# Moving the next batch row's norm statistics into the FFN's first steps, and the FFN's first low part ahead of the second half's mixer addition

## The chip, the cores and the metric

The kernel runs on one core of one Trainium2 chip. The metric is the device time of one execution in microseconds (us). Before the change it is 1379.34 us, the median of 3 runs (1378.56 to 1380.21). The engines are named as the profile names them: PE is TensorE (PEld its weight loads), DVE is VectorE, ACT is ScalarE, POOL is GpSimd, SP is SyncE, which issues most of the DMA transfers.

## What is computed

Four batch rows of 512 tokens by 256 features go through four residual layers: a Mamba2 mixer, an FFN with weights quantized to -1, 0, 1, a causal attention with ALiBi biases, and a mixture of 64 experts. The two layers that the change touches are the first two:

```python
x = x + _L0_attn_ref(_layernorm(x), ...)   # mixer: ... g * rsqrt(mean(g * g) + EPS) * norm_w, then W_out
x = x + _L0_ffn_ref(_layernorm(x), w1, w2, w3)

def _layernorm(x, axis=-1, eps=1e-05):
    m = jnp.mean(x, axis=axis, keepdims=True)
    v = jnp.var(x, axis=axis, keepdims=True)
    return (x - m) / jnp.sqrt(v + eps)

# inside _L0_ffn_ref, with quantized weights
x1 = _bitlinear(x, w1)
x2 = _bitlinear(x, w2)
hidden = jax.nn.sigmoid(x1) * x2
return _bitlinear(hidden, w3)
```

## The kernel before, in words

The order of the work is written out by hand for each engine. Each engine runs its own list of instructions strictly in that order, and the lists meet in semaphores: `at(s, k)` makes the engine wait until signal `s` has been given `k` times in the current batch row `b`; `row(r)` switches `b`, so that a step of the coming batch row can stand among the steps of the present one. The four batch rows go one after the other through mixer, FFN and attention; the experts come at the end for all of them. Tokens are in four tiles of 128 (`T = 4`), and two tiles make a half (`p_` is 0 or 1).

Five normalizations of this kind exist, numbered `n`: 0 ahead of the mixer (its input in `pob`, statistics in `hstats`, `hmv`), 1 ahead of the FFN (`xb`, `stats`, `mv`), 2 ahead of the attention, 3 ahead of the experts. Each goes through four engines:

- `norm_stats(n, t)` on DVE: `bn_stats` of a tile (L1628), then `bn_aggr` (L1630);
- `norm_rstd(n, tiles)` on POOL: add epsilon (L2117), power -0.5 (L2118), for each tile in turn;
- `norm_apply(n, t)` on DVE (L1635): subtract the mean, multiply;
- `norm_T` on PE (L1083) turns a half, and `norm_copy` on ACT (L761) brings it out of PSUM.

For normalization 1 the copy on ACT writes the fp16 high part of the turned activations, and `low_part(p_)` on DVE (L1717) writes what it leaves over. PE's first FFN product waits for `low_part(0)`, and its products from step 6 on for `low_part(1)`.

The end of the mixer does, for each half: `mean_of_squares` (DVE, L1712), the root of it (POOL, L2189, signal `rms_rstd`), `add_mixer` (DVE, L1723 before: two instructions that add the mixer's output to `xb`), statistics and application of normalization 1. POOL takes the means and the statistics in the order in which `mixer_steps` on POOL lists them.

The FFN has 12 steps `n` (six tiles of the hidden layer for each half). In each, PE makes the up products (L1273, 8 matmuls), ACT the sigmoid (L880), DVE the product with the other branch (L1785, "hid" below), ACT its fp16 high part (L882), DVE the low part (L1788), and PE, two steps later, the down products (L1283, 4 matmuls). DVE's product of step `n` comes behind its low part of step `n - 1`. At step 8 DVE adds the first half's FFN output and starts normalization 2.

In batch rows 0 to 2 there is a coming row, whose normalization 0 is done in the shadow of all this. Batch row 3 has none: it runs the same code without the steps of a coming row.

Of the kernel before, what the change touches and what calls it, by code (L numbers as in the profile page):

```python
# [27 lines left out]
T = L // P  # L28
# [95 lines left out]
def build(nc, a, per_row):  # L124


    with ExitStack() as ctx:
# [1474 lines left out]
        def _(dve):  # L1602
# [5 lines left out]
            def at(s, k):  # L1608
                dve.wait_ge(s.sem, s.upto(k, b))

            def row(r):
                nonlocal b
                b = r
# [103 lines left out]
                h_lo_done.inc(v.tensor_tensor(h_lo[:, :, cols], pb[p_][:, :].rearrange("p (k n) -> p k n", k=KD), h_hi[:, :, cols], ALU.subtract))  # L1717

            def add_mixer(p_):
                at(rms_rstd, p_ + 1)  # L1720
                at(out_mm, T * (G - 1) + 2 * p_ + 2)
                for t in range(2 * p_, 2 * p_ + 2):
                    po_read.inc(v.scalar_tensor_tensor(out=xb[:, t, :], in0=pb[6 + p_][:, (t % 2) * D:(t % 2 + 1) * D], scalar=rms[:, t:t + 1],  # L1723
                                                       in1=xb[:, t, :], op0=ALU.mult, op1=ALU.add))
                if p_ == 1:
                    low_part(0)
                for t in range(2 * p_, 2 * p_ + 2):
                    at(po_read, t + 1)
                    norm_stats(1, t)

            def mixer_steps(coming):
                here = b
                for s in range(LAST):
                    _, early, late, _ = ahead_of(s)
                    if s + 1 < UNITS:
                        decays(s + 1, 0)
                    halves_of_y(s)
                    if s + 1 < UNITS:
                        decays(s + 1, 1)
                    gated(s)  # L1740
                    for tile in early:
                        if tile[0] == "x":
                            convolve(tile)
                    if s % T < T - 1:
                        grow_state(s)
                    for tile in late:
                        if tile[0] == "x":
                            convolve(tile)
                at(x_loaded, 1)
                for p_ in range(2):  # L1750
                    mean_of_squares(p_)
                    add_mixer(p_)
                    if coming is not None:
                        row(coming)
                        if p_ == 0:
                            dve.wait_ge(xnext_loaded.sem, xnext_loaded.upto(coming + 1))
                        for t in range(2 * p_, 2 * p_ + 2):
                            norm_stats(0, t)
                        row(here)
                    for t in range(2 * p_, 2 * p_ + 2):  # L1760
                        norm_apply(1, t)

            def ffn(coming):
                here = b
                for n in range(2 * FT):
                    p_, f = divmod(n, FT)
                    if coming is not None and n < T:
                        row(coming)
                        norm_apply(0, n)
                        row(here)  # L1770
                    if n == 3:
                        low_part(1)
                    if n == FT + 2:
                        for t in range(2):
                            add_ffn(t)
# [269 lines left out]
            for r in range(B):  # L2045
                coming = r + 1 if r + 1 < B else None
                row(r)
                mixer_steps(coming)
                ffn(coming)
                first_queries(coming)  # L2050
                attention(coming)
# [44 lines left out]
        def _(pool):  # L2096
# [6 lines left out]
            def row(r):  # L2103
                nonlocal b
                b = r
# [41 lines left out]
            def mixer_steps(done, coming):  # L2147
# [38 lines left out]
                for p_ in range(2):  # L2186
# [1 line left out]
                    settle(pool)  # L2188
                    rms_rstd.inc(p.tensor_tensor(rms[:, 2 * p_:2 * p_ + 2], msv[:, 2 * p_:2 * p_ + 2], power[:, 2 * p_:2 * p_ + 2], ALU.pow))  # L2189
                    norm_rstd(1, [2 * p_, 2 * p_ + 1])  # L2190
                    if coming is not None:
                        row(coming)
                        norm_rstd(0, [2 * p_, 2 * p_ + 1])
                        row(here)

            def maxima_parts(g):
                t, q = AGROUPS[g]
# [145 lines left out]
```

## Time and profile before

| | |
|---|---|
| median of 3 runs | 1379.34 us (1378.56 to 1380.21) |
| profiled execution | 1377.98 us, its span 1376.2 us |
| PE busy | 1146.5 us, 83% of the span |
| DVE busy | 906.0 us, 66% |
| ACT busy | 657.7 us, 48% |
| POOL busy | 585.4 us, 43% |
| mean granted clock of PE | 0.947 of full |

The span runs from the first to the last instruction that the profile shows; the execution's own time is 1.8 us longer. A busy share is an average over very different stages. The change lies in three stretches of about 25 us, one in each of the batch rows 0 to 2 (from about 203, 502 and 799 us on), and in a smaller way in batch row 3 (from 1099 us), so it has to be read from the order of time there.

### The profile page before, as it was taken

Reading aid. Unit: us, or ns where it says so; the run is one execution under the profiler, and the core shown is the slowest. Engines: PE = TensorE matmul, PEld = TensorE weight load, DVE = VectorE, ACT = ScalarE, POOL = GpSimd, SP = SyncE. Lnnn points to the kernel's source line nnn. Section 1 sums busy time; section 2 is a strip of 40 time slices with the busy share of each in tenths; the row PEclk is TensorE's granted clock in tenths of the full one; section 3 lists DMA queues with packets and bytes.
Section 4 is the critical chain, followed back from the end, with each engine's and each line's share of the span. In section 5 each row is a group of like instructions: output and inputs, shape, how many; then the busy total and the mean of one; then the engine's idle time right before and its main releaser. Section 6 shows DMA issues by size and latency. Waiting matters only on the chain.

```text
span 1376.2 us, 24576 instructions
## 1 busy us (share of the span) xinstructions
PE 1146.5 (83%) x8422; PEld 735.4 (53%) x8422; DVE 906.0 (66%) x1846; ACT 657.7 (48%) x1576; POOL 585.4 (43%) x789
## 2 busy tenths in 40 slices
PE   3799997888899978988899978989899978879940
PEld 2355565665555546655555656655555656654520
DVE  4488876655778866655887865656888755561417
ACT  3655523665454515666544335656544245621630
POOL 1254562220387761210677832200777612234750
PEclk9999998999999999998999999999999999989975
DMA  7365542300243304100343332001333525076879
GB/s 311 119 204 195 182 129 73 93 3 20 86 152 113 110 25 118 47 6 31 120 138 109 103 74 70 25 21 44 124 124 114 187 73 162 9 263 205 158 131 370
DMA packets 120139, 159.58 MB, mean 116 GB/s; under 512 B 11632, under 2 KB 82928, under 8 KB 119280
## 3 DMA queue, kind: packets, MB, share of 16 engines
q1 hardware_dynamic: 105232, 129.64, 30.0%
q0 software_dynamic: 9216, 19.98, 5.6%
q10 hardware_dynamic: 5568, 8.39, 1.7%
q8 instruction: 69, 1.13, 0.4%
q14 instruction: 54, 0.44, 0.1%
HBM read 104.55 MB, written 40.83 MB: 106 GB/s over the span
## 4 chain that ended last, share of the span: by engine, by line
PE 46%; DVE 19%; POOL 12%; issue 9%; ACT 8%; DMA 3%; ACTq 1%; POOLq 0%; SPq 0%; DVEq 0%
PE bank L1160 12%; DVE pool_c L1659 5%; PE bank L1202 4%; PE bank L1083 3%; POOL joint L2138 3%; DVE joint L1675 3%; PE bank L1381 3%; PE bank L1340 3%; PE bank L1366 3%; POOL xn L2145 2%; PE bank L1465 2%; PE bank L1305 2%; ACT joint L830 2%; DVE pool_c L1700 2%; PE bank L1181 2%
## 5 line engine op out<-in xcount | busy, mean ns | idle before, releaser
L1160 PE MATMUL bank<-xm,joint 128*128 128x512 f32 x544 | 272.0, 625 | 21.4 <-DVE pool_c L1659 15.6
L2138 POOL TENSOR_TENSOR joint<-joint 128x512 f32<-128x512 f32 x128 | 168.4, 1317 | 246.8 <-DVE joint L1675 246.2
L1659 DVE SCALAR_TENSOR_TENSOR pool_c<-bank,params,pool_c 128x511 f32<-128x511 f32 (+2 forms) x216 | 161.2, 747 | 86.6 <-ACT pool_c L791 81.2
L1160 PEld LDWEIGHTS bank<-xm,joint 128*128 128x128 f32 x544 | 99.8, 197 | 125.8 <-issue 93.3
L1851 DVE TENSOR_REDUCE nmax<-bank 128x1 f32<-128x384 f32 (+3 forms) x176 | 109.6, 638 | 57.3 <-PE bank L1341 56.5
L830 ACT ACTIVATE joint<-bank,dt_ 128x64 f32<-128x64 f32 x512 | 111.7, 342 | 31.1 <-PE bank L1083 31.1
L1202 PE MATMUL bank<-wout,pool_c 128*128 128x256 f32 x512 | 121.8, 381 | 1.2 <-DVE pool_c L1700 1.2
L1202 PEld LDWEIGHTS bank<-wout,pool_c 128*128 128x128 f32 x512 | 95.9, 190 | 33.7 <-issue 22.2
L2132 POOL DMA_INDIRECT xslot<-xrow,slots x96 | 97.0, 1010 | 34.9 <-issue 20.4
L800 ACT ACTIVATE pool_c<-pool_c 128x512 f32<-128x512 f32 x64 | 40.3, 629 | 135.8 <-DVE pool_c L1659 135.8
L1700 DVE TENSOR_TENSOR pool_c<-xn,pool_c 128x512 f32<-128x512 f32 x64 | 90.0, 1406 | 21.5 <-POOL xn L2145 21.5
L953 ACT ACTIVATE pool_c<-bank 128x512 f32<-128x512 f32 (+1 forms) x156 | 83.1, 550 | 17.8 <-PE bank L1368 15.6
L2117 POOL TENSOR_SCALAR vare<-mv 128x1 f32<-128x1 f32 x48 | 9.3, 194 | 190.0 <-DVE mv L1630 186.7
L1675 DVE TENSOR_TENSOR_SCAN joint<-pool_b,bank 128x512 f32<-128x512 f32 x64 | 77.6, 1213 | 17.1 <-POOL pool_b L2172 17.1
L1083 PE MATMUL bank<-consts,pool_c 128*128 128x128 f32 (+1 forms) x368 | 65.1, 278 | 22.3 <-DVE pool_c L1659 15.3
L1181 PEld LDWEIGHTS bank<-joint 128*64 128x64 f32 x1024 | 54.6, 136 | 53.3 <-issue 27.8
L1181 PE MATMUL bank<-joint 128*64 128x128 f32 x1024 | 70.0, 279 | 10.8 <-POOL joint L2138 10.8
L842 ACT ACTIVATE pool_c<-pool_c 128x512 f32<-128x512 f32 x64 | 40.6, 634 | 78.0 <-DVE pool_c L1700 78.0
L791 ACT ACTIVATE pool_c<-bank,params 128x512 f32<-128x512 f32 x72 | 56.4, 783 | 42.7 <-PE bank L1160 42.4
L2145 POOL TENSOR_TENSOR xn<-xn 128x512 f32<-128x512 f32 x48 | 60.8, 1267 | 32.3 <-DVE xn L1688 32.3
L1273 PE MATMUL bank<-pool_c,ffnw 128*128 128x256 f16 x384 | 58.7, 307 | 17.8 <-DVE pool_c L1717 14.0
L1340 PE MATMUL bank<-joint 108*128 108x128 bf16 (+3 forms) x256 | 68.9, 303 | 4.9 <-DVE nmax L1851 4.4
(272 smaller groups left out, 2399.6 us busy)
## 6 DMA issues: line engine op xcount, KB each, us to landing
pool_b<-dA_rows SPq DMA_DIRECT2D x64, 256.0 KB
pool_b<-dec_rows SPq DMA_DIRECT2D x96, 128.0 KB, 3.5
joint<-pool_b SPq DMA_DIRECT2D x96, 128.0 KB, 2.4
acc<-xrow SPq DMA_DIRECT2D x13, 640.0 KB, 6.1
joint<-dA_rows SPq DMA_DIRECT2D x32, 256.0 KB, 3.1
dA_late<-dA_rows SPq DMA_DIRECT2D x32, 256.0 KB, 3.9
xslot<-xrow SPq DMA_DIRECT2D x16, 321.0 KB, 4.7
pool_b<-xslot SPq DMA_DIRECT2D x64, 80.2 KB, 2.5
```

Source lines behind the costliest of these rows:

```text
L830: ins = sa.activation(xdt[g % 2][:, t, j * P + e * HP:j * P + (e + 1) * HP], bank_of(tile)[:, t * P + e * HP:t * P + (e + 1) * HP], ACT.Co ...
L1083: return nc.tensor.transpose(out, in_, ident[0:size, 0:size])
L1160: last = mm(bank[:, :], win[:, k, col:col + P], xm[:, k, :], start=(k == 0), stop=(k == KD - 1))
L1181: last = mm(pb[2][e * HP:(e + 1) * HP, j * P:(j + 1) * P], xdt[g % 2][:, c, h * HP:(h + 1) * HP], M[u % 2][:, h, :], start=True, stop=True)
L1202: last = mm(pb[6 + c // 2][:, (c % 2) * D:(c % 2 + 1) * D], gs[w % 2][:, j * P:(j + 1) * P], wout[:, g * GK + j, :], start=(g == 0 and j = ...
L1340: mm(out, qs[0:ROWS, h0 + i, t * P:(t + 1) * P], ks[0:ROWS, h0 + i, 0:w], start=True, stop=False)
L1659: ins = v.scalar_tensor_tensor(out=cv[:, n:L], in0=bank[:, 0:L - n], scalar=convw[:, ci, TAPS - 1 - n:TAPS - n], in1=cv[:, n:L], op0=ALU.m ...
L1675: L_ready.inc(v.tensor_tensor_scan(Lx[:, half * 4:half * 4 + 4, :].rearrange("p h i -> p (h i)"), dA[u % 2][half], pb[4][:, :], 0.0, ALU.m ...
L1700: g_ready.inc(v.tensor_tensor(gs[u % 2], ys_, szT[g % 2][:, c, :], ALU.mult))
L1851: max_done.inc(v.tensor_reduce(nmax[:, t * AH + h0:t * AH + h0 + nh], src, AX.X, ALU.max, negate=True))
L2132: scattered.inc(p.indirect_dma_start(xslot, bass.IndirectOffsetOnAxis(ap=slots[:, t, k:k + 1], axis=0), xrow[:, t, :], None))
L2138: M_ready.inc(p.tensor_tensor(M[u % 2][:, hs_, :], Lx[:, hs_, :], cbm[:, c * P:(c + 1) * P].unsqueeze(1).to_broadcast([P, 4, P]), ALU.mult))
```

## The change

On DVE, the statistics of the coming row's normalization 0 leave the end of the mixer, where two tiles stood behind each half's own statistics, and go into the FFN's first four steps, one tile a step. Their application moves back by one step, from steps 0 to 3 to steps 1 to 4. `low_part(1)` stays in step 3 but now stands ahead of that step's statistics. `low_part(0)` moves ahead of the two additions of the second half, and with them ahead of their wait for `rms_rstd`. On POOL the coming row's roots move behind both halves.

```diff
@@ DVE @@
             def add_mixer(p_):
+                if p_ == 1:
+                    low_part(0)
                 at(rms_rstd, p_ + 1)
                 at(out_mm, T * (G - 1) + 2 * p_ + 2)
                 for t in range(2 * p_, 2 * p_ + 2):
                     po_read.inc(v.scalar_tensor_tensor(out=xb[:, t, :], in0=pb[6 + p_][:, (t % 2) * D:(t % 2 + 1) * D], scalar=rms[:, t:t + 1],
                                                        in1=xb[:, t, :], op0=ALU.mult, op1=ALU.add))
-                if p_ == 1:
-                    low_part(0)
...
                     add_mixer(p_)
-                    if coming is not None:
-                        row(coming)
-                        if p_ == 0:
-                            dve.wait_ge(xnext_loaded.sem, xnext_loaded.upto(coming + 1))
-                        for t in range(2 * p_, 2 * p_ + 2):
-                            norm_stats(0, t)
-                        row(here)
                     for t in range(2 * p_, 2 * p_ + 2):
                         norm_apply(1, t)
...
+                    if n == 3:
+                        low_part(1)
                     if coming is not None and n < T:
                         row(coming)
-                        norm_apply(0, n)
+                        if n == 0:
+                            dve.wait_ge(xnext_loaded.sem, xnext_loaded.upto(coming + 1))
+                        norm_stats(0, n)
+                        if n >= 1:
+                            norm_apply(0, n - 1)
                         row(here)
-                    if n == 3:
-                        low_part(1)
+                    elif coming is not None and n == T:
+                        row(coming)
+                        norm_apply(0, T - 1)
+                        row(here)
@@ POOL @@
                     norm_rstd(1, [2 * p_, 2 * p_ + 1])
-                    if coming is not None:
-                        row(coming)
-                        norm_rstd(0, [2 * p_, 2 * p_ + 1])
-                        row(here)
+                if coming is not None:
+                    row(coming)
+                    norm_rstd(0)
+                    row(here)
```

DVE's own order at the end of the mixer and into the FFN's first step, as one piece of the difference (the same in batch rows 0, 1 and 2; `stats` and `mv` belong to the present row, `hstats` and `hmv` to the coming one, L1785 and L1788 are hid and its low part):

```order
 L1635 TENSOR_SCALAR xn<-xb,mv,rstd 128x256 x2
 L1712 TENSOR_SCALAR msv<-bank 128x2
-L1723 SCALAR_TENSOR_TENSOR xb<-bank,rms,xb 128x256 x2
 L1717 TENSOR_TENSOR pool_c<-bank,pool_c 128x2x256
-L1628 BN_STATS stats<-xb 128x6
-L1630 BN_AGGR mv<-stats 128x2
-L1628 BN_STATS stats<-xb 128x6
-L1630 BN_AGGR mv<-stats 128x2
-L1628 BN_STATS hstats<-pob 128x6
-L1630 BN_AGGR hmv<-hstats 128x2
-L1628 BN_STATS hstats<-pob 128x6
-L1630 BN_AGGR hmv<-hstats 128x2
+L1725 SCALAR_TENSOR_TENSOR xb<-bank,rms,xb 128x256 x2
+L1628 BN_STATS stats<-xb 128x6
+L1630 BN_AGGR mv<-stats 128x2
```

The first low part (L1717) now stands directly behind the mean of squares, and the additions (L1723, now L1725) follow it; two pairs for `hstats` are gone from between the present row's statistics and their application.

POOL's order at the same place (`rms` is the root of the mean of squares, `vare` and `rstd` belong to the present row, `hvare` and `hrstd` to the coming one):

```order
-L2117 TENSOR_SCALAR hvare<-hmv 128x1
-L2118 TENSOR_TENSOR hrstd<-hvare,power 128x1
-L2117 TENSOR_SCALAR hvare<-hmv 128x1
-L2118 TENSOR_TENSOR hrstd<-hvare,power 128x1
-L2189 TENSOR_TENSOR rms<-msv,power 128x2
-L2117 TENSOR_SCALAR vare<-mv 128x1
-L2118 TENSOR_TENSOR rstd<-vare,power 128x1
-L2117 TENSOR_SCALAR vare<-mv 128x1
-L2118 TENSOR_TENSOR rstd<-vare,power 128x1
+L2189 TENSOR_TENSOR rms<-msv,power 128x2
```

The second half's `rms` (L2189) no longer has two tiles of the coming row ahead of it on POOL. The lists of PE, ACT and SP are the same before and after.

## Rows read from the trace of the kernel before

**Rows 1.** The page, part 4: the chain that ended last, by engine.

```profile
PE 46%; DVE 19%; POOL 12%; issue 9%; ACT 8%; DMA 3%; ACTq 1%; POOLq 0%; SPq 0%; DVEq 0%
```

**Rows 2.** Timeline, POOL, batch row 0: start, duration, engine, line, [idle before <-releaser].

```profile
210.41 0.69 POOL L2189 TENSOR_TENSOR rms<-msv,power 128x2 f32<-128x2 f32 x1 [0.20 <-POOL hrstd L2118]
...
214.97 0.55 POOL L2118 TENSOR_TENSOR rstd<-vare,power 128x1 f32<-128x1 f32 x1 [0.18 <-POOL vare L2117]
```

**Rows 3.** Timeline, DVE, batch row 0, end of the mixer.

```profile
208.22 0.15 DVE L1712 TENSOR_SCALAR msv<-bank 128x2 f32<-128x2 f32 x1
211.14 0.88 DVE L1723 SCALAR_TENSOR_TENSOR xb<-bank,rms,xb 128x256 f32<-128x256 f32 x2 [2.77 <-POOL rms L2189]
211.93 0.68 DVE L1717 TENSOR_TENSOR pool_c<-bank,pool_c 128x512 f16<-128x512 f32 x1
...
213.09 0.18 DVE L1630 BATCH_NORM_AGGREGATE mv<-stats 128x2 f32<-128x6 f32 x1
...
214.47 0.40 DVE L1628 BATCH_NORM_STATS2 hstats<-pob 128x6 f32<-128x256 f32 x1
...
215.10 0.87 DVE L1635 TENSOR_SCALAR xn<-xb,mv,rstd 128x256 f32<-128x256 f32 x2
215.89 0.41 DVE L1635 TENSOR_SCALAR pob<-pob,hmv,hrstd 128x256 f32<-128x256 f32 x1
```

**Rows 4.** Timeline, ACT, batch row 0: the two copies of normalization 1.

```profile
208.84 0.60 ACT L761 ACTIVATE pool_c<-bank 128x512 f16<-128x512 f32 x1 [1.40 <-PE bank L1083]
...
220.12 0.58 ACT L761 ACTIVATE pool_c<-bank 128x512 f16<-128x512 f32 x1
```

**Rows 5.** Timeline, DVE, batch row 0, FFN: hid of steps 0, 2, 3, 4, 7.

```profile
216.21 0.42 DVE L1785 TENSOR_TENSOR pool_c<-bank,pool_c 128x256 f32<-128x256 f32 x1
...
219.34 0.42 DVE L1785 TENSOR_TENSOR pool_c<-bank,pool_c 128x256 f32<-128x256 f32 x1
...
220.91 0.68 DVE L1717 TENSOR_TENSOR pool_c<-bank,pool_c 128x512 f16<-128x512 f32 x1
221.51 0.41 DVE L1785 TENSOR_TENSOR pool_c<-bank,pool_c 128x256 f32<-128x256 f32 x1
...
222.75 0.42 DVE L1785 TENSOR_TENSOR pool_c<-bank,pool_c 128x256 f32<-128x256 f32 x1
...
226.70 0.42 DVE L1785 TENSOR_TENSOR pool_c<-bank,pool_c 128x256 f32<-128x256 f32 x1
```

**Rows 6.** Timeline, PE, batch row 0, FFN: up products of steps 5 and 6.

```profile
221.98 1.05 PE L1273 MATMUL bank<-pool_c,ffnw 128*128 128x256 f16 x8 [0.57 <-DVE pool_c L1785]
...
223.41 1.04 PE L1273 MATMUL bank<-pool_c,ffnw 128*128 128x256 f16 x8
```

**Rows 7.** Timeline, DVE, batch row 3: the second half's mixer addition.

```profile
1105.29 0.88 DVE L1723 SCALAR_TENSOR_TENSOR xb<-bank,rms,xb 128x256 f32<-128x256 f32 x2 [0.90 <-POOL rms L2189]
```

**Rows 8.** Timeline, ACT, batch row 3: the first half's copy of normalization 1.

```profile
1104.85 0.60 ACT L761 ACTIVATE pool_c<-bank 128x512 f16<-128x512 f32 x1 [1.49 <-PE bank L1083]
```

**Rows 9.** One line of the program, L1788: durations in ns, minimum, median, maximum.

```profile
L1788 DVE TENSOR_TENSOR pool_c<-pool_c x48: 424/426/427, 217.1 to 1131.9; 128x256 f16<-128x256 f32 x48
```

**Rows 10.** Timeline, PE, batch row 0: from normalization 2's turning to the first query product.

```profile
232.70 1.11 PE L1083 MATMUL bank<-consts,xn 128*128 128x128 f32 x4 [2.62 <-DVE xn L1635]
...
237.54 1.97 PE L1305 MATMUL bank<-xnT,pool_c 128*128 128x256 f32 x8
```

**Rows 11.** Timeline, PE, batch row 1: the same two places.

```profile
531.32 0.75 PE L1083 MATMUL bank<-consts,xn 128*128 128x128 f32 x4 [2.62 <-DVE xn L1635]
...
534.96 1.32 PE L1305 MATMUL bank<-xnT,pool_c 128*128 128x256 f32 x5 [0.27 <-ACT xnT L761]
```

**Rows 12.** Windows: length, busy of PE, PEld, DVE, ACT, POOL; PE's clock, DMA share, GB/s.

```profile
210.00:211.00 1.00, 0.00 (x0) 0.00 (x0) 0.00 (x0) 0.00 (x0) 0.80 (x2) 0.50 0.00 0
...
234.00:235.00 1.00, 1.00 (x7) 0.70 (x5) 0.20 (x1) 0.23 (x1) 0.00 (x0) 0.50 0.00 0
532.00:533.00 1.00, 1.00 (x11) 0.89 (x10) 0.43 (x1) 0.86 (x3) 0.00 (x0) 1.00 0.00 0
```

More of the change, by code:

```diff
@@ L1729, in add_mixer, with mixer_steps @@
                     norm_stats(1, t)
-            def mixer_steps(coming):
-                here = b
+            def mixer_steps():
                 for s in range(LAST):
@@ L2047, in _ @@
                 row(r)
-                mixer_steps(coming)
+                mixer_steps()
                 ffn(coming)
```

## The prediction

> **What bounds the kernel now.** I read the page first: PE has the largest part of the chain that ended last, then DVE, and POOL is in it with 12% [rows 1]. No engine is the bound everywhere, so I read the timeline of each engine where the change lies. Times are of batch row 0; batch rows 1 and 2 repeat its spacings at the end of the mixer and through the FFN's first steps to a few hundredths.
>
> At the end of the mixer DVE and POOL hand work to each other. DVE has the second mean of squares at 208.22, and then stands idle for 2.77 us until `rms`, which POOL starts only at 210.41, because it first takes two tiles of the coming row: its releaser is `hrstd` [rows 2, 3]. The first low part runs at 211.93, behind the additions, though the copy that it needs ended at 208.84 + 0.60 = 209.44 [rows 3, 4]. PE is idle meanwhile and waits for that low part.
>
> In the FFN, PE is not the pace. A step of DVE is hid, a wait for ACT's copy, the low part, and again hid: 222.75 - 221.51 = 1.24 us when nothing else is in it [rows 5]. DVE is strictly in order, so that what is put ahead of hid lengthens the step, while its short wait inside cannot be filled by it. The reader should see that two different things end the two waits: PE waits for the low part (early work), while DVE is already late at hid of step 0.
>
> **The change, part by part.**
>
> *Low part first, `rms` first.* After the change POOL is free for `rms` when the mean of squares is there. From msv at 208.22 + 0.15, a root of 0.69 and some 0.2 of handing over, `rms` is there at about 209.3 [rows 2, 3]. That is ahead of the copy's end at 209.44, so the copy decides: the low part starts at 209.47 instead of 211.93, and PE's first product with it, 2.46 us earlier. The two additions follow the low part. Additions, low part and the first statistics took 213.09 - 211.14 = 1.95 us in the old order and take it in the new; so the first `mv` comes at 209.47 + 1.95 = 211.42, 1.67 us earlier [rows 3].
>
> *Application of the second half.* It ended by POOL: the last `rstd` ended at 214.97 + 0.55 = 215.52 [rows 2], and DVE's two applications, 0.87 us with a wait in them, ended with the next instruction at 215.89 [rows 3]. The two pairs for `hstats` that stood ahead of them (214.47 to 215.10, so 0.63 us each) lay in that same wait for POOL. They cost DVE nothing where they were, and taking them away brings only what POOL brings, 1.67 us: DVE is free at 214.22.
>
> *Statistics in the steps.* There the four pairs are in the open. One stands ahead of hid of step 0: the first application of the coming row (0.32 us, 215.89 to 216.21 [rows 3, 5]) leaves that place, so hid starts at 214.22 + 0.63 = 214.85, 1.36 us earlier than 216.21. Its sigmoid is long there, since PE began 2.46 us earlier. Steps 1, 2 and 3 each have a pair more and as many applications as before: + 3 x 0.63 = + 1.89. In step 3 the second low part now stands first. It needs ACT's copy, which ended at 220.12 + 0.58 = 220.70, 1.36 us behind hid of step 2; DVE would get there 1.25 us behind it (1.57, 219.34 to 220.91, less the 0.32 of the application now behind it), so it waits 0.14 [rows 4, 5]. Hid of step 3 is then at -1.36 + 1.89 + 0.14 = + 0.67. Step 4 takes the fourth application: + 0.32, so + 0.99.
>
> *What the FFN gives back.* Between steps 4 and 7 there is a little slack. Hid of step 7 came at 226.70, while three free steps from 222.75 end at 226.47: 0.23. On PE, the up product of step 5 starts 0.47 behind hid of step 3, and that of step 6 starts 0.66 behind hid of step 4 [rows 5, 6]: 0.19. The smaller one counts: + 0.80 us at step 7. From there DVE goes straight on to the first half's addition and normalization 2, for which PE waits 2.62 us [rows 10], so nothing is left to take it up, and the rest of the batch row is later by 0.80.
>
> *POOL's roots and the queues.* The coming row's roots follow one step behind the statistics and are used a step later still; a step (1.24 + 0.32 + 0.63) is longer than the way through POOL. SP's loads of late weights wait for the last application and start 1.67 us earlier, in no one's way. No DMA is added or moved past another. These cost nothing; if the cover of the roots went, an `hrstd` would come late by its own 0.55 us in a step.
>
> *Batch row 3* has no coming row. The additions started at 1105.29; the low part, now ahead of them, can start when the copy is there, 1104.85 + 0.60 + 0.03 = 1105.48 [rows 7, 8]. The additions and statistics move back by 0.19, and here POOL paces too: + 0.2 us.
>
> **Sum:** 3 x 0.80 + 0.2 = + 2.6 us. Against the profiled execution's 1377.98 that is 1380.6; the median is 1.36 above the profiled one, so the forecast is 1379.34 + 2.6 = 1381.9 us. A measurement of this kernel can tell about 0.2% (2.8 us) from no change, and the forecast lies just inside it.
>
> *A resource that the old rows show only in part.* POOL's roots will now run beside DVE's low parts L1788, which read two SBUF tensors. L1788 took 424 to 427 ns in all 48 executions, some of them beside roots on POOL and most not [rows 9]. So I price it at 0. The Trainium skill, "GPSIMD Engine Reference", section "Specifications", says that GpSimd shares its SBUF interfaces with VectorE, with contention when the DVE instruction has two SBUF inputs. By it the sum would be larger than by the row; the trace so far doesn't bear it out for this pair.
>
> **Rivals.**
>
> *1. PE's clock gives some of it back.* In batch row 0 the granted clock was 0.50 (1.2 GHz) from 234 on, after PE had stood idle for 2.62 us; in batch row 1, after an idle time of the same length, it was 1.00 (2.4 GHz) [rows 10 to 12]. From the turning to the first query product it took 4.84 us in the first (232.70 to 237.54) and 3.64 in the second (531.32 to 534.96): 1.20 us [rows 10, 11]. A shift of 0.8 us can move such a spell on or off the busy stretch, by luck. One spell fewer makes + 1.4 us, 1380.7; two fewer + 0.2. For it: the same idle time ends both ways. Against: it can also go the other way. The Trainium skill, "TensorE: Matmul & The Clock Gate", section "What's actually happening", says that the throttled state is the default and activity releases it. The trace agrees as far as both levels follow idle time.
>
> *2. Slower by more.* PE starts earlier, and then waits for hid of step 0 with only two up products done. At 210 to 211 the clock was 0.50 [rows 12]. If it stays low through the longer first steps, products that took 1.04 us take nearly twice that, and DVE, which now has 0.14 of waiting in step 3, waits for PE as well. Bounds: nothing, since a step is now about 2.2 us and PE needs less even at the low level; and the 1.20 of a low spell in each of three rows, + 3.6. With POOL and DVE in each other's way at one root of 0.55 in four steps of three rows the bound would be + 6.6, to which I give a few in a hundred. I take + 1.8, half the first: 1383.7 us.
>
> *3. Faster.* The early start reaches the end: if the waits of DVE in the steps took in the pairs (if hid were set by PE or by the sigmoid), only the 1.36 us at step 0 would count: - 3 x 1.36 + 0.2 = - 3.9, 1375.4 us. It decides as soon as less than 1.36 of the four steps' additions (1.89 + 0.14 + 0.32, less the 0.2 of slack) is in the open. For it: PE and ACT do start 2.46 earlier. Against: hid follows its own predecessor on DVE directly in rows 5, with no idle time named.
>
> *4. It does nothing.* The 0.8 us is swallowed further on by something that has its own time, a transfer for one: DMA is 3% of the chain [rows 1]. 1379.3 us. Against: these transfers are themselves started by the chain.
>
> **How the numbers follow.** Forecast (+ 1.8 to + 3.6, since each term is good to 0.1 or 0.2 and there are three of each): 47 in 100. Rival 1: 20. Rival 2: 18. Rival 3: 6. Rival 4: 9. About half of the forecast's share lies beyond 0.2%, and so does nearly all of rival 2, and some of both mixed: slower 0.44, same 0.49, faster 0.07. The range for 8 in 10 leaves out rival 3, part of 4 and the far end of 2: 1379.0 to 1385.2 us.
>
> **What the profile after would show.** Right: the low part some 0.03 behind the copy's end, 1.2 us behind msv; `rms` no longer waited for by more than a moment; hid of step 0 1.36 us nearer to msv (6.63 instead of 7.99 us), hid of step 3 0.67 and of step 7 0.80 us farther (14.0 and 19.3); in steps 1 to 3 a spacing of 2.2 us; DVE's L1788 still at 426 ns. Wrong: steps 0 to 3 ended by PE or ACT in the releasers of L1785 (rival 2 or 3); a period from one batch row's msv to the next's that differs from before by more than 0.8 us in either direction, with the clock in the windows to tell why (rival 1); L1788 longer, or hid 7 at its forecast place and the period unchanged (rival 4).

## The result, and the profile after

The changed kernel takes 1383.34 us (median of 7 runs, 1380.49 to 1385.51), the kernel before 1378.56 (7 runs on the same chip, 1376.60 to 1380.21). The ratio is 1.0039, with a 95% interval of 1.0028 to 1.0049: slower, by about 5.4 us by the ratio and 4.8 by the medians. The forecast was 1381.9 in a range of 1379.0 to 1385.2. So the direction and the range hold, and the size is roughly double the + 2.6 forecast; the median lies above the + 1.8 to + 3.6 of the forecast's own mechanism, in the part of the range that rival 2 had opened.

The profiled execution took 1385.28 us (span 1383.4), which is at the upper end of the seven. Its part 4, beside [rows 1]:

```profile
PE 48%; DVE 20%; POOL 10%; issue 8%; ACT 8%; DMA 2%; ACTq 1%; SPq 0%; POOLq 0%; DVEq 0%
```

POOL has gone from 12 to 10% of the chain: that part of the change works. PE and DVE have risen (46 to 48%, 19 to 20%). On POOL, in batch row 0, `rms` now starts 0.17 behind the mean of squares instead of 2.04 ([rows 2, 3] for before):

```profile
209.58 0.70 POOL L2189 TENSOR_TENSOR rms<-msv,power 128x2 f32<-128x2 f32 x1 [0.68 <-DVE msv L1712]
...
214.16 0.28 POOL L2117 TENSOR_SCALAR vare<-mv 128x1 f32<-128x1 f32 x1 [0.22 <-POOL rstd L2118]
214.62 0.54 POOL L2118 TENSOR_TENSOR rstd<-vare,power 128x1 f32<-128x1 f32 x1 [0.18 <-POOL vare L2117]
```

DVE, batch row 0, end of the mixer and steps 0 to 4 and 7 of the FFN; it answers to [rows 3] and [rows 5]:

```profile
203.94 0.15 DVE L1712 TENSOR_SCALAR msv<-bank 128x2 f32<-128x2 f32 x1
...
209.26 0.15 DVE L1712 TENSOR_SCALAR msv<-bank 128x2 f32<-128x2 f32 x1
210.69 0.69 DVE L1717 TENSOR_TENSOR pool_c<-bank,pool_c 128x512 f16<-128x512 f32 x1 [1.28 <-ACT pool_c L761]
211.30 0.87 DVE L1725 SCALAR_TENSOR_TENSOR xb<-bank,rms,xb 128x256 f32<-128x256 f32 x2
...
215.20 0.41 DVE L1635 TENSOR_SCALAR xn<-xb,mv,rstd 128x256 f32<-128x256 f32 x1 [0.81 <-POOL rstd L2118]
215.53 0.42 DVE L1628 BATCH_NORM_STATS2 hstats<-pob 128x6 f32<-128x256 f32 x1
216.09 0.18 DVE L1630 BATCH_NORM_AGGREGATE hmv<-hstats 128x2 f32<-128x6 f32 x1
216.20 0.42 DVE L1785 TENSOR_TENSOR pool_c<-bank,pool_c 128x256 f32<-128x256 f32 x1
...
218.41 0.42 DVE L1785 TENSOR_TENSOR pool_c<-bank,pool_c 128x256 f32<-128x256 f32 x1
...
220.62 0.42 DVE L1785 TENSOR_TENSOR pool_c<-bank,pool_c 128x256 f32<-128x256 f32 x1
...
222.00 0.69 DVE L1717 TENSOR_TENSOR pool_c<-bank,pool_c 128x512 f16<-128x512 f32 x1
...
223.57 0.42 DVE L1785 TENSOR_TENSOR pool_c<-bank,pool_c 128x256 f32<-128x256 f32 x1
...
225.13 0.41 DVE L1785 TENSOR_TENSOR pool_c<-bank,pool_c 128x256 f32<-128x256 f32 x1
...
229.02 0.42 DVE L1785 TENSOR_TENSOR pool_c<-bank,pool_c 128x256 f32<-128x256 f32 x1
```

To read: the low part starts with the copy and the additions behind it. A pair of statistics ends, and hid follows at once (216.09, 216.20): the pair is in the open. The first three hids stand 2.21 us apart, where 1.57 was the spacing before.

PE, batch row 0, the first up products, those of step 5, the turning for normalization 2 and the first query product; it answers to [rows 6, 10]:

```profile
211.53 3.57 PE L1273 MATMUL bank<-pool_c,ffnw 128*128 128x256 f16 x16 [1.50 <-DVE pool_c L1717]
216.68 1.89 PE L1273 MATMUL bank<-pool_c,ffnw 128*128 128x256 f16 x8 [1.58 <-DVE pool_c L1785]
...
224.04 1.05 PE L1273 MATMUL bank<-pool_c,ffnw 128*128 128x256 f16 x8 [1.34 <-DVE pool_c L1785]
...
235.02 0.75 PE L1083 MATMUL bank<-consts,xn 128*128 128x128 f32 x4 [2.62 <-DVE xn L1635]
...
238.66 1.97 PE L1305 MATMUL bank<-xnT,pool_c 128*128 128x256 f32 x8 [0.26 <-ACT xnT L761]
```

**Where the time is.** The profiled executions can be cut at the first mean of squares of each batch row (before 202.99, 501.58, 798.74, 1098.91; after 203.94, 502.63, 803.60, 1103.30) and at the turning for normalization 2. The first difference is the stretch that the change touches, the second all that follows it:

| stretch | mean of squares to turning, before → after | turning to the next row's mean of squares (row 3: to the end) |
|---|---|---|
| batch row 0 | 29.71 → 31.08: + 1.37 | 268.88 → 267.61: - 1.27 |
| batch row 1 | 29.74 → 30.91: + 1.17 | 267.42 → 270.06: + 2.64 |
| batch row 2 | 29.72 → 30.91: + 1.19 | 270.45 → 268.79: - 1.66 |
| batch row 3 | 27.00 → 27.21: + 0.21 | 250.29 → 252.89: + 2.60 |

That is + 3.94 in the touched stretch, + 2.31 behind it and + 0.95 ahead of batch row 0. The last two are in places where the program is the same. Part of the second difference (- 1.20 in row 0, + 1.18 in row 1) lies between the turning and the first query product, which came 4.84 us behind the turning in row 0 and 3.64 in row 1 before, and 3.64 and 4.82 after. The windows from 6.00 us behind the turning to the next row's mean of squares (row 3: to the end; columns as in [rows 12]) show what differs further on. The kernel before, batch rows 1, 2 and 3:

```profile
537.32:798.74 261.42, 236.10 (x1773) 151.43 (x1771) 187.48 (x353) 139.19 (x335) 122.39 (x165) 0.98 0.25 79
834.46:1098.91 264.45, 239.16 (x1780) 153.46 (x1778) 187.60 (x354) 139.56 (x335) 122.37 (x165) 0.97 0.29 91
1131.91:1376.20 244.29, 170.80 (x1500) 105.15 (x1498) 117.70 (x364) 91.71 (x208) 90.74 (x132) 0.86 0.64 183
```

And the changed kernel:

```profile
539.54:803.60 264.06, 240.84 (x1780) 155.17 (x1778) 187.80 (x354) 139.65 (x335) 122.56 (x165) 0.96 0.25 78
840.51:1103.30 262.79, 237.41 (x1780) 152.43 (x1778) 187.83 (x354) 139.65 (x335) 122.55 (x165) 0.98 0.29 91
1136.51:1383.40 246.89, 174.72 (x1498) 108.44 (x1498) 117.66 (x364) 91.90 (x208) 90.86 (x132) 0.84 0.64 181
```

DVE, ACT and POOL do the same work in the same time (in rows 1 and 2 DVE 187.5 to 187.8, ACT 139.2 to 139.7, POOL 122.4 to 122.6). PE's busy time alone moves, up where the clock is lower (0.98 to 0.96, and in row 3 0.86 to 0.84) and down where it is higher (0.97 to 0.98), and the length goes with it. Over the execution, windows of half a microsecond, each counted by its share at the low level, sum to 147 us there before and 167 after. The seven executions of the changed kernel fit this: the two shortest (1380.49 and 1380.54) have a mean clock of 0.945, the longest (1385.51 and 1385.28) 0.941 and 0.940. Lowest against lowest is 1380.49 - 1376.60 = 3.89, close to the 3.94 of the first column, though two single executions are a weak comparison.

### The profile page after: what moved, and what is told of

The parts are those of the page before. It is cut to its first block, busy times and chain, and to the rows that moved or that the text cites. A ratio compares the mean times of both kernels' runs of the same rounds, so it can differ in the third digit from the quotient of the medians.

```text
span 1383.4 us, 24574 instructions
## 1 busy us (share of the span) xinstructions
PE 1157.9 (84%) x8420; PEld 743.1 (54%) x8422; DVE 906.9 (66%) x1846; ACT 658.5 (48%) x1576; POOL 586.1 (42%) x789
## 4 chain that ended last, share of the span: by engine, by line
PE 48%; DVE 20%; POOL 10%; issue 8%; ACT 8%; DMA 2%; ACTq 1%; SPq 0%; POOLq 0%; DVEq 0%
PE bank L1160 12%; DVE pool_c L1659 5%; PE bank L1083 4%; PE bank L1202 4%; PE bank L1381 3%; POOL joint L2138 3%; DVE joint L1675 3%; PE bank L1340 3%; PE bank L1366 2%; POOL xn L2145 2%; PE bank L1305 2%; PE bank L1465 2%; PE bank L1181 2%; PE bank L1196 2%; PE bank L1457 2%
```

## The experiments

In the expectations "turning" is the start of PE's turning for normalization 2, counted from the row's first mean of squares; a sum of turnings is taken over the four batch rows, against the kernel before. Each of these numbers comes from one profiled execution of the kernel. Times are medians with their number of runs; the kernel before is 1378.39 us (24 runs) beside e1 to e4, and named for the others.

**One part alone.** Two kernels have one part of the change each. `e1_low_only` is the kernel before with

```
 def add_mixer(p_):
+    if p_ == 1:
+        low_part(0)
     at(rms_rstd, p_ + 1)
     ...
-    if p_ == 1:
-        low_part(0)
```

> The low part of the first half ahead of the second half's additions, and nothing else; the coming row's statistics and roots stay as before. Theory (DVE's chain sets the rows): in batch rows 0 to 2 the root of the second half is still late behind two tiles of the coming row, so the additions stay at msv + 8.2 us, the low part lies in that wait (msv + 6.5), and only its 0.6 us leaves the way behind the additions: hid of step 0 at msv + 12.6 instead of 13.2, the turning for normalization 2 about 0.6 earlier in each of three rows, 0.2 later in batch row 3. Sum - 1.6 us. Rival (the early low part itself brings a loss, since PE starts early and then stands at its low clock): turning not earlier, hid of step 2 or 3 waiting for PE or ACT, the sum 0 to + 1.5 us.

`e2_stats_only` is the changed kernel with exactly that edit taken back.

> The coming row's statistics in the FFN's steps and its roots behind both halves, but the first low part behind the additions as before. Theory: DVE pays for the pairs in the steps; the additions can start at msv + 6.4, the low part follows, hid of step 0 at msv + 11.9, hid of step 4 at 20.8, the turning for normalization 2 at 30.7 (before: 29.7; changed kernel: 30.9). Sum 3 x 1.0 and nothing in batch row 3: + 3.0 us, some 0.8 us less than the changed kernel. Rival (the early low part is a gain in the changed kernel, which offsets the statistics): turning later than 30.9 + 0.2, sum over + 4.5.

Measured: e1 1382.78 us (12 runs, 1378.00 to 1387.79), ratio 1.0033 (1.0019 to 1.0048); its turnings sum to + 0.02. e2 1384.96 us (7 runs), ratio 1.0041 (1.0027 to 1.0056); its turnings sum to + 3.21, where + 3.0 was expected; its time is + 5.7 us by the ratio. In e2's batch row 1 (mean of squares at 502.64), DVE's low part and hid of step 0, and then PE's turning:

```profile
509.82 0.68 DVE L1717 TENSOR_TENSOR pool_c<-bank,pool_c 128x512 f16<-128x512 f32 x1
...
514.53 0.42 DVE L1785 TENSOR_TENSOR pool_c<-bank,pool_c 128x256 f32<-128x256 f32 x1
```

```profile
533.34 0.76 PE L1083 MATMUL bank<-consts,xn 128*128 128x128 f32 x4 [2.62 <-DVE xn L1635]
```

Hid of step 0 comes 11.89 and the turning 30.70 behind the mean of squares. The statistics in the steps, together with POOL's new order, have the loss without the early low part. In the changed kernel, low part first makes the turning 30.91 instead of e2's 30.70, so 0.2 us worse in each of rows 1 and 2, and not the cause of it. e1 is a surprise: it should have gained 1.6 us and lost 4.4. Its rival had the turning right (not earlier) but allowed only + 1.5 us. Its batch row 1 (mean of squares at 502.7), PE:

```profile
510.03 3.57 PE L1273 MATMUL bank<-pool_c,ffnw 128*128 128x256 f16 x16 [1.50 <-DVE pool_c L1717]
515.82 1.89 PE L1273 MATMUL bank<-pool_c,ffnw 128*128 128x256 f16 x8 [2.22 <-DVE pool_c L1785]
```

and DVE, two hids of steps further on, where PE rather than DVE sets the pace:

```profile
522.14 0.42 DVE L1785 TENSOR_TENSOR pool_c<-bank,pool_c 128x256 f32<-128x256 f32 x1
...
523.45 0.42 DVE L1785 TENSOR_TENSOR pool_c<-bank,pool_c 128x256 f32<-128x256 f32 x1
```

PE starts early with two steps' products (16), then stands idle for 2.22 us until hid of step 0, and the next eight take 1.89 us instead of 1.05: low clock (the window of these products stands further down). It falls behind, and the steps are 1.31 us apart instead of the 1.24 of [rows 5]. Hid of step 0 is 0.6 us early, and yet in batch rows 1 and 2 the turning is late by 0.07 and 0.03; in row 0 0.28 of the 0.6 is left. That takes away the expected gain. The loss of 4.4 us itself, with turnings that sum to + 0.02, lies outside the touched stretch, with a clock of 0.945 in e1's shortest execution (1378.00) and 0.931 in its longest.

**The statistics kept in the mixer.** `e3_stats_stay` is the changed kernel with the statistics of the coming row back behind each half's normalization, and POOL's roots and the applications one step later as in the changed kernel:

```
 add_mixer(p_)
+if coming is not None:
+    row(coming)
+    ...
+    for t in range(2 * p_, 2 * p_ + 2):
+        norm_stats(0, t)
+    row(here)
 ...
-                        if n == 0:
-                            dve.wait_ge(xnext_loaded.sem, xnext_loaded.upto(coming + 1))
-                        norm_stats(0, n)
```

> The changed kernel, but the coming row's statistics stay on DVE at the end of the mixer as before; POOL takes their roots behind both halves, and they are applied one step later. Theory (the pairs cost nothing in the wait for POOL, and 0.63 each in the steps): hid of step 0 at msv + 11.4 instead of 13.2 before and 12.1 in the changed kernel, hid of step 4 at 18.4, the turning at 28.3, 1.4 earlier than before in each of three rows, 0.2 later in batch row 3. Sum - 4.0 us against before, 0.3% faster. Rival (the loss of the changed kernel lies in the clock or in the early low part, not in the place of the statistics): the turning at 30.5 or later, sum + 2 or more.

`e4_stats_stay_low_behind` has in addition the first low part behind the additions, as before. Against the kernel before it is (the lines `row(coming)` and `row(here)` are left out)

```
+                    if n == 3:
+                        low_part(1)
                     if coming is not None and n < T:
-                        norm_apply(0, n)
+                        if n >= 1:
+                            norm_apply(0, n - 1)
-                    if n == 3:
-                        low_part(1)
+                    elif coming is not None and n == T:
+                        norm_apply(0, T - 1)
 ... POOL
                     norm_rstd(1, [2 * p_, 2 * p_ + 1])
-                    if coming is not None:
-                        norm_rstd(0, [2 * p_, 2 * p_ + 1])
+                if coming is not None:
+                    norm_rstd(0)
```

> As the run with the statistics kept in the mixer and the roots behind both halves, but with the first low part behind the additions as before. Theory: since the root is then no longer late, the low part ahead of the additions makes DVE wait for ACT's copy, and behind them it does not: turning at 28.1, 0.2 earlier than with the low part first, in all four rows; sum - 4.8 us against before. Rival (PE's early start is worth something): turning later than with the low part first, sum - 3.5 or less gain.

Measured: e3 1374.96 us (11 runs), ratio 0.9975 (0.9966 to 0.9984), turnings - 3.99. e4 1372.82 us (5 runs), ratio 0.9956 (0.9943 to 0.9969), turnings - 5.33. Expected were - 4.0 and - 4.8. DVE of e4, batch row 1 (mean of squares at 500.36), with the pairs in its wait for POOL and hid of steps 0 and 1:

```profile
506.66 0.88 DVE L1723 SCALAR_TENSOR_TENSOR xb<-bank,rms,xb 128x256 f32<-128x256 f32 x2 [0.90 <-POOL rms L2194]
...
509.35 0.40 DVE L1628 BATCH_NORM_STATS2 hstats<-pob 128x6 f32<-128x256 f32 x1
...
509.99 0.39 DVE L1628 BATCH_NORM_STATS2 hstats<-pob 128x6 f32<-128x256 f32 x1
...
510.63 0.87 DVE L1635 TENSOR_SCALAR xn<-xb,mv,rstd 128x256 f32<-128x256 f32 x2
511.41 0.42 DVE L1790 TENSOR_TENSOR pool_c<-bank,pool_c 128x256 f32<-128x256 f32 x1
...
512.98 0.41 DVE L1790 TENSOR_TENSOR pool_c<-bank,pool_c 128x256 f32<-128x256 f32 x1
```

and its turning on PE:

```profile
528.30 1.12 PE L1083 MATMUL bank<-consts,xn 128*128 128x128 f32 x4 [2.62 <-DVE xn L1635]
```

This is the reading that settles the cause. From the changed kernel to e3 the only edit is the place of four pairs; the turning goes from 30.91 to 28.13 in rows 1 and 2, 2.78 us for each (2.36 in row 0), and the time from + 0.39% to - 0.25%. The part of the change that is good is POOL's order, and its gain is to be had if the pairs stay where they fill DVE's wait: in e4 hid of step 0 comes 11.05 behind the mean of squares instead of 13.24. Of these 2.19 us some 0.32 are the coming row's application, which has left step 0 here too. POOL's order with the applications in their old steps was not run.

**How much each pair costs.** `e5_two_pairs` is e4 with the second half's two pairs moved into steps 1 and 2:

```
-                    if coming is not None:
+                    if coming is not None and p_ == 0:
 ...
+                        if n in (1, 2):
+                            norm_stats(0, n + 1)
```

> The kernel with the statistics kept in the mixer, the roots behind both halves and the low part behind the additions, but with the statistics of the second half's two tiles moved into steps 1 and 2 of the FFN: two pairs in the steps instead of none or four. Theory (0.64 us for each pair, and nothing gained where they were): hid of step 1 at msv + 13.3 instead of 12.6, hid of step 4 at 19.3 instead of 18.05, the turning at 29.2 instead of 27.95; sum + 3.8 us against that kernel, that is - 1.5 against before. Rival (the pairs' cost lies in what they do to PE's clock): turning unmoved or up by less than 0.6.

`e6_second_low_last` is e4 with the second low part behind step 3's application:

```
-                    if n == 3:
-                        low_part(1)
                     if coming is not None and n < T:
 ...
+                    if n == 3:
+                        low_part(1)
```

> The kernel with the statistics kept in the mixer, the roots behind both halves and the first low part behind the additions, with the second low part of step 3 behind that step's application again. Theory (ahead of it DVE waits 0.14 us for ACT's copy): hid of step 3 and the turning 0.14 earlier (27.8), sum - 0.4 us against that kernel, not to be told in the time. Rival (DVE waits for nothing there, or PE paces step 3): no change of the turning.

Measured, with the kernel before at 1377.82 us (28 runs): e5 1378.18 us (12 runs), ratio 0.999 (0.9977 to 1.0002), turning at 29.30 in rows 1 and 2, where e4 has 27.94: + 1.35 for two pairs, 0.67 each. The sum of e5's turnings is - 1.12, where - 1.5 was expected. e6 1375.00 us (11 runs), ratio 0.9976 (0.9967 to 0.9985), turning at 27.80: - 0.15. DVE of e5, batch row 1, hid of steps 0 and 1 with the statistics ahead of that of step 1:

```profile
512.09 0.42 DVE L1792 TENSOR_TENSOR pool_c<-bank,pool_c 128x256 f32<-128x256 f32 x1
...
513.33 0.42 DVE L1628 BATCH_NORM_STATS2 hstats<-pob 128x6 f32<-128x256 f32 x1
...
514.29 0.42 DVE L1792 TENSOR_TENSOR pool_c<-bank,pool_c 128x256 f32<-128x256 f32 x1
```

A step with a pair takes 2.20 us. Hid of step 0 stands 11.14 behind the mean of squares (512.09 - 500.95) with two pairs less in the mixer, and 11.05 in e4 with all four there: in the mixer they cost nothing. And each of the two pairs costs as much as each of the four did: the cost is by the pair. e6 moved the turning as expected, yet its time is 2.2 us above e4's, at a mean clock of 0.938 to 0.943 against 0.949. So a difference of some tenths of a us in the turning cannot be told from this kernel's time.

**PE's clock.** These kernels record more products on PE, of constants into a bank that is not read, so that PE is busy in three of its waits. They leave all that is computed as it was:

```
                 norm_T(1, 0)
+                stay_awake(3, pb[4])
 ...
+                    if n == 2:
+                        stay_awake(3, pb[4])
 ...
                     if n == FT + 3:
+                        stay_awake(8, pb[4])
                         norm_T(2, 0)
```

`f1_before_filled` adds this to the kernel before, `f2_after_filled` to the changed one, `f3_low_only_filled` to e1 and `f4_best_filled` to e4.

> The kernel before with products that nobody reads in three idle stretches of PE in each batch row's FFN: 3 behind the first turning, 3 ahead of the up products of step 2, 8 ahead of the turning for normalization 2. Nothing of the computation changes. Both theories: the low spell behind normalization 2 (1.2 us in batch rows 0, 2 and 3) goes away: about - 3 us, if the added products (0.22 us each at the high clock) fit into the idle stretches of 4.0, 0.7 and 2.6 us.

> The changed kernel with the same added products. Theory (the changed kernel's loss is DVE's chain, 3.9 us by the turnings, plus 1 to 2 us of PE's clock): against the kernel before with the same products it stands at + 3.9 us, the turnings at + 1.2, and the time by each batch row's period differs by the turning alone. Rival (the loss behind the turnings has another cause than the clock): + 5 us or more against the filled kernel before, with full clock in the FFN.

> The early low part alone, with the same added products. Theory (its + 4.4 us are PE's clock: PE starts early, stands idle until hid of step 0, runs the next products at the low clock and falls behind DVE): with PE kept busy the 0.6 us of each batch row come through, turnings 0.6 earlier than in the filled kernel before, sum - 1.6 us against it. Rival (the order itself costs): still + 3 us or more against it.

> Statistics kept in the mixer, roots behind both halves, low part behind the additions, with the same added products. Theory: - 5.3 us against the filled kernel before, as the turnings say. Rival (part of its gain without the products was the clock's): - 3 to - 4 us against it.

`f5_low_only_three` is e1 with only the three products ahead of step 2.

> The early low part alone, with only 3 products that nobody reads, ahead of the up products of step 2, in PE's idle stretch of 1.5 to 2.2 us there. Theory (the early start lets PE's clock stay low into steps 2 to 4, and then PE paces the steps at 1.31 us): the pace from step 4 to 6 is again 1.24, hid of step 7 at msv + 23.15 instead of 23.8, the turning at 29.2 instead of 29.8; time - 1.6 to - 2.5 us against the same kernel without them. Rival (PE is behind for another reason): pace 1.31, turning at 29.8.

Measured, f1 to f4 beside 1377.89 us (24 runs) of the kernel before, f5 beside 1377.82:

| kernel | median us (runs) | ratio (95%) | sum of turnings |
|---|---|---|---|
| f1 | 1374.05 (8) | 0.9973 (0.9962 to 0.9983) | + 0.81, all in row 3 |
| f2 | 1378.21 (11) | 1.0003 (0.9994 to 1.0012) | + 3.79 |
| f3 | 1375.23 (11) | 0.9985 (0.9973 to 0.9996) | - 1.50 |
| f4 | 1370.80 (5) | 0.9943 (0.9930 to 0.9957) | - 5.04 |
| f5 | 1375.87 (11) | 0.9982 (0.9973 to 0.9991) | - 1.64 |

f5 in batch row 1 (mean of squares at 504.31), PE with the unread products in the second line (the trace has two of the three), and then two hids of DVE:

```profile
511.64 3.33 PE L1276 MATMUL bank<-pool_c,ffnw 128*128 128x256 f16 x16 [1.50 <-DVE pool_c L1721]
515.02 0.59 PE L1221 MATMUL bank<-consts,identb 128*128 128x512 bf16 x2
517.43 1.05 PE L1276 MATMUL bank<-pool_c,ffnw 128*128 128x256 f16 x8 [1.82 <-DVE pool_c L1789]
```

```profile
523.49 0.42 DVE L1789 TENSOR_TENSOR pool_c<-bank,pool_c 128x256 f32<-128x256 f32 x1
...
524.73 0.42 DVE L1789 TENSOR_TENSOR pool_c<-bank,pool_c 128x256 f32<-128x256 f32 x1
```

Windows of the eight up products of step 2 in the two kernels, e1 and then f5 (the clock is the third number from the end):

```profile
515.82:517.71 1.89, 1.89 (x9) 1.33 (x10) 1.09 (x3) 1.01 (x3) 0.85 (x3) 0.50 0.81 230
```

```profile
517.43:518.48 1.05, 1.05 (x9) 0.79 (x10) 0.62 (x2) 0.67 (x2) 0.65 (x3) 1.00 0.30 107
```

With three unread products in each batch row the clock is 1.00 where it was 0.50, the eight products take 1.05 us instead of 1.89, the steps are 1.24 apart instead of 1.31, and the turning comes at 29.13, as expected. So e1's lost gain was PE's clock: low part first brings its 0.6 us for each row at the turning. But the trace does not show the unread products raising the clock in this row. It had risen before they began, at 515.02; f5 again:

```profile
514.00:515.00 1.00, 0.96 (x6) 0.68 (x6) 0.82 (x4) 0.00 (x0) 0.60 (x2) 0.71 0.00 0
515.00:516.00 1.00, 0.59 (x2) 0.10 (x1) 0.74 (x4) 0.00 (x0) 0.60 (x3) 1.00 0.00 0
```

In e1's batch row 2 the clock rose in the same place, fell again in the wait, and half of the next products were slow (1.46 us for eight); what filling may do there is keep the clock up. How much of the difference between e1 and f5 is that, and how much is where each execution happened to stand, one profile of each does not settle.

The time falls from 1382.78 to 1375.87, by 6.9 us, where 1.6 to 2.5 were expected; the turnings have 1.66 of it, and the rest lies outside the stretch, with the clock (0.931 to 0.945 in e1's executions, 0.946 to 0.948 in f5's). Against the equally filled kernel before, low part first still does not win in time: f3 takes 1.2 us more than f1, where 1.6 less was expected and the rival said 3 more, although its turnings sum to 2.31 less. 0.58 of these are in batch row 3, where the unread products themselves had made f1 later.

Filling takes 3.8 us off the kernel before and 5.1 off the changed one, so it does not explain the loss away: between f1 and f2, both filled, there are 4.2 us by the medians (3.0 by the turnings), near the + 3.9 expected. In f1 the first query product comes 3.64 us behind the turning in all four rows, so the low spells of rows 0, 2 and 3 are gone, as expected. For f4 the expected 5.3 us below f1 became 3.3, with 5.85 by the turnings; that is what its rival said, and part of e4's gain without the filling may have been the clock's.

## Why the prediction was right in sign and short in size

**POOL's order, right.** `rms` is waited for no more than a moment, the low part starts with the copy, and the second half's application comes earlier. Hid of step 0 came 12.26, 12.09 and 12.09 behind the first mean of squares in rows 0 to 2, against 13.24: - 0.96, - 1.17, - 1.15, where the step "hid starts at 214.85, 1.36 us earlier" had - 1.36. This term was mis-sized by 0.2, and by 0.4 in batch row 0. The second mean of squares itself is 0.09 later, and POOL's `vare` ahead of the last root took 0.28 us instead of 0.19. The first half's `vare` ahead of its last root did the same (0.28 at 207.89, before 0.19 at 206.93), which accounts for the 0.09; why it takes longer is open. In batch row 0 PE's turning for normalization 1 was at the low clock besides, 0.63 us, and the low part came 1.43 behind the second mean of squares instead of the 1.25 of the other rows.

**The pairs, right.** This was the working's main term: in the mixer they lie in a wait, in the steps they are in the open. Steps with a pair took 2.21 us (forecast 2.2), 0.64 more each. From hid of step 0 to that of step 3 it is 7.37 us, before 5.30 (in each case rows 1 and 2 within 0.02): + 2.07, forecast 1.89 + 0.14 = 2.03. e3 (2.78 per row by the turning) and e5 (0.67 for a pair) show it as the cause, and e2 shows that it suffices.

**The fourth application, right;** 1.57 from hid 3 to hid 4 in rows 1 and 2 instead of 1.24: + 0.33, forecast + 0.32.

**The give-back, wrong in size.** "The smaller one counts: + 0.80 us at step 7" had 0.19 us of slack taken up. The three steps from hid 4 to hid 7 went from 3.96 to 3.89: 0.07. Hid of step 7 waits for PE in both kernels: it starts 0.50 and 0.51 us behind the end of step 7's up products. These are the up products of step 7 before,

```profile
225.16 1.04 PE L1273 MATMUL bank<-pool_c,ffnw 128*128 128x256 f16 x8
```

and in the changed kernel:

```profile
227.47 1.04 PE L1273 MATMUL bank<-pool_c,ffnw 128*128 128x256 f16 x8
```

They stand 2.41 behind hid of step 4 before (222.75) and 2.34 after (225.13). The prediction took PE's order between the two for slack that would close by 0.19: the up products of step 6 were to start 0.47 behind hid of step 4 instead of 0.66, and they started 0.56 behind it (225.69). So the term that was mis-sized is the slack on PE, 0.07 where the sum had 0.19. With the other terms this makes the turning + 1.18 in rows 1 and 2 and + 1.37 in row 0, instead of + 0.80: about 0.2 of the miss (0.4 in row 0) from hid of step 0, 0.1 from the give-back. **Batch row 3**: + 0.21, forecast + 0.2.

By the turnings the sum is thus + 3.94 instead of + 2.6. The rest up to the ratio's + 5.4, some 1.5 us, is not in the touched stretch, and the sum had no term for it. In the profiled pair the time outside the stretch goes with PE's clock in places where the program is unchanged, both signs occurring; its cause is open.

**Rival 1** (the clock gives back) had its spell right and its balance wrong. The low spell at normalization 2 did move: batch row 0 lost it (235.02 to 238.66, 3.64 us) and row 1 gained it. PE in batch row 1 of the changed kernel, beside [rows 11]:

```profile
533.54 1.01 PE L1083 MATMUL bank<-consts,xn 128*128 128x128 f32 x4 [2.62 <-DVE xn L1635]
...
538.36 1.89 PE L1305 MATMUL bank<-xnT,pool_c 128*128 128x256 f32 x8
```

It takes 4.82 us from the turning to the query product. The prediction's sign for rival 1, a period that differs by more than 0.8 us, came in this row alone: 297.16 us before, 300.97 after. Three rows of four have the spell, after (4.82, 4.84, 4.88 us from the turning to the first query product) as before (4.84, 4.88, 4.88), so nothing was given back on balance. **Rival 2** (slower by more, through the clock) is in part what happened: the size is its 1383.7 nearly to the number, but that is luck, since the place it named, the first steps, does little in the changed kernel. A step is so long there that PE at the low clock keeps up: the first hids are 2.21 apart in batch row 0, where eight products take 1.89 us, and in row 1, where they take 1.05. It is e1, with short steps, that shows rival 2's mechanism. The extra low clock of the profiled execution lies mostly from 6 us behind the turnings of rows 1 and 3 on (+ 10.3 and + 9.8 us of it, by the windows of half a microsecond), in no changed code. Which of its spells comes from the change, and which from where an execution happens to stand, the runs don't settle: filling the three waits leaves a difference of the same size. **Rival 3** (the early start reaches the end) falls with e2 and the changed kernel: low part first gives nothing there. **Rival 4** falls with the ratio.

The row of L1788 in the changed kernel, beside [rows 9]:

```profile
L1788 DVE TENSOR_TENSOR pool_c<-pool_c x48: 424/425/427, 217.1 to 1136.5; 128x256 f16<-128x256 f32 x48
```

It stayed the same, so the price of 0 was right, but it was hardly put to the test: in the changed kernel the coming row's roots run beside L1788 only once in each of the batch rows 0 to 2, for 0.27 us, and 0.19 to 0.21 before. There it starts as soon behind hid (0.91 us) as in the steps without that (0.90) and takes 0.42 us like the rest. The contention for which the Trainium skill, "GPSIMD Engine Reference", section "Specifications", names this kind of instruction is not seen in these rows; whether it would be with more of both side by side, no run shows.

The best of the versions tried is e4's order with the filled waits: 1370.80 us, 0.57% below the kernel before; without filling 1372.82, 0.44% below. In each case the comparison is with the kernel before without filling.

## What to carry to other kernels

Work done inside a wait cost nothing there and cost its full time where the engine is never idle, so a change that moves work must say which wait it leaves and which it enters; a change that shortens that wait at the same time (here POOL's order) should be tried without the move. Count a moved operation at each place as "in a wait" or "in the open", instead of by engine. Where a kernel alternates between short bursts and waits on PE, compare executions of like mean clock, or compare offsets between two fixed points of the profile, before a difference of 0.3% is put down to the edit.

## What the runs showed of the hardware

An earlier start of PE can lengthen its low-clock time: in batch row 1 of e1 a burst of 3.57 us, then 2.22 us idle, was followed by products at 1.2 GHz (1.89 us for eight) and a pace set by PE. It need not: with the same early start the changed kernel's batch row 1 has its clock up by the end of the burst (3.47 us) and takes 1.05 us for the eight. With three unread products in that wait the kernel takes 6.9 us less, 1.66 of them by the turnings. The Trainium skill, "TensorE: Matmul & The Clock Gate", section "What's actually happening", says that the throttled level is the default and that activity releases it; e1 and f5 agree as far as both levels occur behind like work, clock 0.50 and 1.00 at the products of step 2, but f5's clock had risen ahead of the added products.

The time of one and the same kernel mostly goes with the mean granted clock of the execution: e1 took 1378.0 us at 0.945 and 1387.8 at 0.931, and e5's twelve runs fall into two groups, about 1373 to 1375 us at 0.951 to 0.953 and 1378 to 1380 at 0.943 to 0.949. Between kernels the clock can move against the edit: e6, with turnings 0.15 us earlier than e4's, took 2.2 us more, at 0.938 to 0.943 against 0.949. That the shift of 0.15 us brought this on is not shown.
